# Causal attention: the mask on the scores' diagonal blocks moves from TensorE products to GpSimd selects on the exponentials

## The reference

```
sa, ca, ga, sb, cb, gb = (mod[:, 0], ..., mod[:, 5])
h = _layernorm(x) * (1 + ca) + sa
q, k, v = heads(Wq, bq), heads(Wk, bk), heads(Wv, bv)          # 16 heads of 16
att = einsum('bhtd,bhsd->bhts', q, k) * scale
att = where(causal, att, -inf)
y = einsum('bhts,bhsd->bhtd', softmax(att), v) -> (B, T, C) @ Wp + bp
x = x + ga * y
h = _layernorm(x) * (1 + cb) + sb
x = x + gb * ffn(h)                                            # two layers, untouched
```

## Time and profile before

| | |
|---|---|
| time, 3 runs | 4161.38 us median, 4150.5 to 4162.23 |
| profiled execution | 4156.13 us, its span 4154.3 us |
| busy in the span | PE 3759.8 (91%), DVE 3079.0 (74%), ACT 2612.0 (63%), POOL 1887.2 (45%) |
| mean granted PE clock | 0.964 |
| L728 ACT exponentials | 768, 610.9 us busy; 528.5 us idle before them, 371.7 of it until L869 |
| L907 / L882 / L924 PE | 1536 / 1536 / 3072 products |

### The profile page before, as it was taken

How to read it: one execution, slowest core, us unless ns; L and a number is a source line. 1 busy time by engine, 2 the same in 40 slices (tenths; PEclk the granted TensorE clock), 3 DMA queues, 4 the chain that set the end, 5 groups by cost and what they waited for, 6 DMA issues and landing times.

```text
span 4154.3 us, 88049 instructions
## 1 busy us (share of the span) xinstructions
PE 3759.8 (91%) x33070; PEld 2895.4 (70%) x33070; DVE 3079.0 (74%) x7229; ACT 2612.0 (63%) x5759; POOL 1887.2 (45%) x1444
## 2 busy tenths in 40 slices
PE   4799999999998759999999999989999999999997
PEld 2354545445544347888888888878888888888886
DVE  4677777777776358777787877777888788788884
ACT  1355555555555447777777777767777777767774
POOL 1212322232233035555555555555666565656664
PEclk7799999999999879999999999999999999999999
DMA  4444244353441120000000000011000000000000
GB/s 124 88 74 119 58 112 102 73 125 75 92 128 34 33 67 31 15 20 18 17 20 15 20 17 18 17 43 41 22 28 27 23 26 22 26 24 25 24 23 21
DMA packets 146019, 195.93 MB, mean 47 GB/s; under 512 B 21596, under 2 KB 119608, under 8 KB 145600
## 3 DMA queue, kind: packets, MB, share of 16 engines
q1 hardware_dynamic: 145600, 190.31, 18.4%
HBM read 113.66 MB, written 67.16 MB: 44 GB/s over the span
## 4 chain that ended last, share of the span: by engine, by line
PE 24%; DVE 14%; ACT 12%; DMA 8%; issue 5%; POOL 0%; DVEq 0%; SPq 0%; POOLq 0%; ACTq 0%
PE b_bank_m L1914 10%; DMA b_hs<-b_fr 8%; PE b_bank_p L1914 5%; ACT b_e L1794 4%; DVE b_e L2142 3%; PE b_bank_et L1979 2%; PE b_bank_t L1914 2%; DVE b_qk_rot L2111 2%; ACT L1837 2%; DVE b_rot L2115 2%; PE b_bank_ot L1994 2%; PE b_bank_s L1968 1%; ACT b_e_t L1804 1%; DVE b_ag L2206 1%; ACT b_ag L1829 1%
## 5 line engine op out<-in xcount | busy, mean ns | idle before, releaser
L728 ACT ACTIVATE a_e_t<-a_ring 128x1024 f32<-128x1024 f32 (+3 forms) x768 | 610.9, 809 | 528.5 <-PE a_ring L869 371.7
L1050 DVE TENSOR_REDUCE a_mx<-a_ring 128x2 f32<-128x1024 f32 (+3 forms) x768 | 724.5, 956 | 233.8 <-PE a_ring L869 113.1
L1682 POOL TENSOR_TENSOR b_e<-b_e,b_share 128x512 f32<-128x512 f32 (+1 forms) x512 | 505.9, 991 | 801.2 <-DVE b_share L2150 801.1
L1794 ACT ACTIVATE b_e<-b_e,b_bias 128x256 f32<-128x256 f32 (+1 forms) x1024 | 494.2, 486 | 164.7 <-DVE b_bias L2142 163.8
L2142 DVE CUSTOM_DVE_ANT_0 b_e<-b_bank_s,b_mask,b_inv 128x256 f32<-128x256 f32 (+1 forms) x1024 | 415.8, 460 | 31.1 <-PE b_bank_s L1968 31.1
L1667 POOL TENSOR_TENSOR b_qk_rot<-b_qk_rot,b_rot 128x512 f32<-128x512 f32 x256 | 351.7, 1384 | 130.1 <-DVE b_rot L2115 130.1
L1804 ACT ACTIVATE b_e_t<-b_bank_et 128x512 f32<-128x512 f32 (+1 forms) x512 | 287.2, 561 | 184.2 <-PE b_bank_et L1979 184.1
L882 PE MATMUL a_ring<-a_k_st,a_q_st 48*128 48x512 f32 (+3 forms) x1536 | 328.2, 424 | 77.4 <-ACT a_e_t L728 41.6
L907 PE MATMUL a_ring<-a_q_st,a_k_st 50*128 50x512 f32 (+3 forms) x1536 | 340.0, 441 | 40.7 <-ACT a_e_t L728 13.7
L907 PEld LDWEIGHTS a_ring<-a_q_st,a_k_st 50*128 50x128 f32 x1536 | 147.5, 189 | 298.0 <-issue 145.0
L1979 PE MATMUL b_bank_et<-b_ident,b_e 128*128 128x128 f32 x1920 | 310.8, 282 | 43.1 <-ACT b_e_t L1804 43.1
(11 more groups left out here) (238 smaller groups left out, 11010.3 us busy)
## 6 DMA issues: line engine op xcount, KB each, us to landing
a_q_st<-a_parts_q SPq DMA_DIRECT2D x192, 128.0 KB, 4.8
a_k_st<-a_parts_k SPq DMA_DIRECT2D x192, 128.0 KB, 7.5
a_parts_q<-a_qk_p SPq DMA_DIRECT2D x16, 1024.0 KB, 8.0
a_parts_k<-a_qk_p SPq DMA_DIRECT2D x16, 1024.0 KB, 8.1
b_fl<-f_rows SPq DMA_DIRECT2D x64, 256.0 KB, 4.1
a_xl<-in_L_attn_x SPq DMA_DIRECT2D x9, 1024.0 KB, 5.3
a_x<-in_L_attn_x SPq DMA_DIRECT2D x8, 1024.0 KB, 9.3
x_rows<-a_x SPq DMA_DIRECT2D x8, 1024.0 KB, 4.6
```

The lines of the kernel that those rows point to most:

```text
L728: act.activation(e_t[:, step % 2, 2 * pair:2 * pair + 2, 0:cols], slot[:, :].rearrange("p (h t) -> p h t", h=2)[:, :, 0:cols], ACT.Exp).th ...
L1050: dve.reduce_max(mx[:, g % 2, :, pair, piece, t:t + 1], slot[:, :].rearrange("p (r c) -> p r c", r=2)[:, :, 0:cols], AX.X)\
L1682: pool.tensor_tensor(weights, weights, share[:, h % SPS, 2 * j:2 * j + 2].unsqueeze(2) .broadcast_to([P, 2, 2 * WIN - lo]), ALU.mult).then ...
L1794: ins = act.activation(weights, weights, ACT.Exp, scale=-1.0, bias=bias[:, h % SPS, at:at + 1], accum_out=total[:, h % SPS, at:at + 1])
```

## The change

The scores of the second pass get no mask products any more: L869 with `mask_st`, four for each pair of each diagonal step, 2048 in all. The exponential is taken of unmasked scores in the triangle. Then POOL sets the masked half of the first 128 columns of both heads to zero in `e_t`, with one `affine_select` per pair (`clear_future`), and `meet_values` of a diagonal step waits for both (`cleared`). The first pass keeps its mask.

POOL's other work, until now in a few long instructions, is cut into pieces and put between the selects by step: 16 scale pieces (8 `tensor_scalar` of 256 columns, 4 products and 4 sums of 512), at `PIECES_AT`, for the f rows of the turn before in group 1 and for x in group 3; the bias in four pieces in steps 8 to 11 of group 2; the sums with the output in steps 6 and 8 of group 0, each half in two instructions. The f rows of a turn are thus modulated in group 1 from step 1 to step 11, and the bias comes in group 2, after the load that follows them. The table `mask_st`, its `memset` and its two selects go, as do the signals `x_scaling` and `f_scaling`. The two waits on `const_made` for 16 become 13.

```
@@ -258,6 +258,15 @@
 STEPS1 = score_steps()
 NSTEP = len(STEPS1)
 LAST = G1 - 1
+DIAGONALS = [n for n, (half, s) in enumerate(STEPS1) if s >= 4 * half]
+NDIAGONAL = len(DIAGONALS)
+
+SCALE_PIECES = 16
+SCALED = 12
+PIECES_AT = (0, 1, 1, 1, 2, 2, 2, 2, 1, 1, 1, 2)
+BIAS_AT = ((2, 8), (2, 9), (2, 10), (2, 11))
+ROWS_AT = ((0, 6), (0, 8))
+assert sum(PIECES_AT) == SCALE_PIECES and len(PIECES_AT) == NSTEP
...
-        mask_st = sb("a_mask_st", [P, 2, P], BF16)
...
-        x_scaling = sig("a_x_scaling", 1)
-        x_scaled = sig("a_x_scaled", 2)
+        x_scaled = sig("a_x_scaled", SCALED)
...
+        cleared = sig("a_cleared", 2 * G1 * NDIAGONAL)
...
-            pool.memset(mask_st[:, :, :], 0.0).then_inc(const_made, 1)
...
-                for m, op, fill, sign in ((ident_h, ALU.not_equal, 1.0, 1), (mask_ts, ALU.is_ge, MASKED, 1),
-                                          (mask_st, ALU.is_ge, MASKED, -1)):
-                    pool.wait_ge(const_made, 10 + 3 * r + (0 if m is ident_h else 1 if m is mask_ts else 2))
+                for m, op, fill in ((ident_h, ALU.not_equal, 1.0), (mask_ts, ALU.is_ge, MASKED)):
+                    pool.wait_ge(const_made, 9 + 2 * r + (0 if m is ident_h else 1))
                     pool.affine_select(out=m[rows, :, :], in_=m[rows, :, :], compare_op=op, fill=fill, base=0,
-                                       pattern=[[64 * sign, 2], [-sign, P]], channel_multiplier=sign)\
-                        .then_inc(const_made, 1)
+                                       pattern=[[64, 2], [-1, P]], channel_multiplier=1).then_inc(const_made, 1)
...
-            def modulate(dst, src, name, shift, scale, scaling, scaled, done, a):
+            def modulate(dst, src, name, shift, scale, scaled, done, k, a):
 
                 aggr, rstd = norms[name]["aggr"], norms[name]["rstd"]
-                pool.wait_ge(rstd_of[name].sem, rstd_of[name].at(a, 1))
-                pool.sem_inc(scaling.sem, 1)
-                for t in range(TB):
-                    ins = pool.tensor_scalar(dst[:, t, :], src[:, t, :], aggr[:, t, 0:1], rstd[:, t:t + 1],
-                                             ALU.subtract, ALU.mult)
-                ins.then_inc(scaled.sem, 1)
-                pool.wait_ge(scaled.sem, scaled.at(a, 1))
-                pool.tensor_tensor(dst[:, :, :], dst[:, :, :], scale.broadcast_to([P, TB, C]), ALU.mult)\
-                    .then_inc(scaled.sem, 1)
-                pool.wait_ge(scaled.sem, scaled.at(a, 2))
-                pool.tensor_tensor(dst[:, :, :], dst[:, :, :], shift.broadcast_to([P, TB, C]), ALU.add)\
-                    .then_inc(done.sem, 1)
-
-            def modulate_x(a):
-                pool.wait_ge(mod_in_loaded.sem, mod_in_loaded.at(a, 1))
-                modulate(xl, xl, "x", mod_in[:, 0:1, :], mod_in[:, 1:2, :], x_scaling, x_scaled, h_ready, a)
-
-            pool.sem_inc(x_scaled.sem, 2)
-            pool.sem_inc(x_scaling.sem, 1)
-            modulate_x(1)
-
-            def body(i, closing=False):
-                pool_steps.start(pool, i)
-                pool.wait_ge(mod_loaded.sem, mod_loaded.at(i, 1))
-                pool.wait_ge(xr_loaded.sem, xr_loaded.at(i, 1))
-                pool_steps.step(pool.tensor_tensor(gate_bp[:, 0, :], modb[:, 0, :], b_p[:, :], ALU.mult))
-                pool.tensor_tensor(x1[:, :, :], x1[:, :, :], gate_bp[:, :, :].broadcast_to([P, TB, C]),
-                                   ALU.add).then_inc(biased.sem, 1)
-                if not closing:
-                    modulate_x(i + 2)
+                ts = slice(2 * (k % 4), 2 * (k % 4) + 2)
+                if k < TB:
+                    pool.wait_ge(rstd_of[name].sem, rstd_of[name].at(a, 1))
+                    pool.tensor_scalar(dst[:, k, :], src[:, k, :], aggr[:, k, 0:1], rstd[:, k:k + 1],
+                                       ALU.subtract, ALU.mult).then_inc(scaled.sem, 1)
+                elif k < SCALED:
+                    pool.wait_ge(scaled.sem, scaled.at(a, TB))
+                    pool.tensor_tensor(dst[:, ts, :], dst[:, ts, :], scale.broadcast_to([P, 2, C]), ALU.mult)\
+                        .then_inc(scaled.sem, 1)
+                else:
+                    pool.wait_ge(scaled.sem, scaled.at(a, SCALED))
+                    ins = pool.tensor_tensor(dst[:, ts, :], dst[:, ts, :], shift.broadcast_to([P, 2, C]), ALU.add)
+                    if k == SCALE_PIECES - 1:
+                        ins.then_inc(done.sem, 1)
+
+            def modulate_x(k, a):
+                if k == 0:
+                    pool.wait_ge(mod_in_loaded.sem, mod_in_loaded.at(a, 1))
+                modulate(xl, xl, "x", mod_in[:, 0:1, :], mod_in[:, 1:2, :], x_scaled, h_ready, k, a)
+
+            def modulate_f(k, a):
+                modulate(f_t, x1, "f", modb[:, 1:2, :], modb[:, 2:3, :], f_scaled, f_done, k, a)
+
+            def clear_future(g, n, a):
+
+                for pair in range(2):
+                    _, _, back, k = slot_of(("s", g, n, pair))
+                    pool.wait_ge(back.sem, back.at(a, k + 1))
+                    block = e_t[:, (g * NSTEP + n) % 2, 2 * pair:2 * pair + 2, 0:P]
+                    pool.affine_select(out=block, in_=block, compare_op=ALU.is_ge, fill=0.0, base=0,
+                                       pattern=[[0, 2], [1, P]], channel_multiplier=-1).then_inc(cleared.sem, 1)
+
+            def add_bias(q, i):
+                if q == 0:
+                    pool_steps.start(pool, i)
+                    pool.wait_ge(mod_loaded.sem, mod_loaded.at(i, 1))
+                    pool.wait_ge(xr_loaded.sem, xr_loaded.at(i, 1))
+                    pool_steps.step(pool.tensor_tensor(gate_bp[:, 0, :], modb[:, 0, :], b_p[:, :], ALU.mult))
+                    pool_steps.end()
+                ts = slice(2 * q, 2 * q + 2)
+                ins = pool.tensor_tensor(x1[:, ts, :], x1[:, ts, :], gate_bp[:, :, :].broadcast_to([P, 2, C]), ALU.add)
+                if q == 3:
+                    ins.then_inc(biased.sem, 1)
+
+            def add_rows(p, i):
                 pool.wait_ge(biased.sem, biased.at(i, 1))
-                for p in range(1 if closing else 2):
-                    pool.wait_ge(gated.sem, gated.at(i, 2 * p + 2))
-                    half = slice(4 * p, 4 * p + 4)
-                    pool.tensor_tensor(x1[:, half, :], x1[:, half, :], f_t[:, half, :], ALU.add)\
-                        .then_inc(x1_done.sem, 1)
-                if closing:
+                pool.wait_ge(gated.sem, gated.at(i, 2 * p + 2))
+                for q in range(2):
+                    ts = slice(4 * p + 2 * q, 4 * p + 2 * q + 2)
+                    ins = pool.tensor_tensor(x1[:, ts, :], x1[:, ts, :], f_t[:, ts, :], ALU.add)
+                ins.then_inc(x1_done.sem, 1)
+
+            def program(mode, i):
+                if mode == "lead":
+                    for k in range(SCALE_PIECES):
+                        modulate_x(k, 1)
+                for g, a in groups(mode, i):
+                    for n in range(NSTEP):
+                        if n in DIAGONALS:
+                            clear_future(g, n, a)
+                        before = sum(PIECES_AT[:n])
+                        for k in range(before, before + PIECES_AT[n]):
+                            if g == 1 and i > 0:
+                                modulate_f(k, i - 1)
+                            if g == 3 and mode == "body":
+                                modulate_x(k, i + 2)
+                        if (g, n) in BIAS_AT:
+                            add_bias(BIAS_AT.index((g, n)), i)
+                        if mode == "body" and (g, n) in ROWS_AT:
+                            add_rows(ROWS_AT.index((g, n)), i)
+                if mode == "closing":
+                    add_rows(0, i)
                     rows, shape = f_t[:, END:TB, :], [P, TB - END, C]
                     pool.wait_ge(end_scaled, 1)
                     pool.tensor_tensor(rows, rows, modb[:, 2:3, :].broadcast_to(shape), ALU.mult)\
                         .then_inc(end_scaled, 1)
                     pool.wait_ge(end_scaled, 2)
                     pool.tensor_tensor(rows, rows, modb[:, 1:2, :].broadcast_to(shape), ALU.add).then_inc(end_done, 1)
-                else:
-                    modulate(f_t, x1, "f", modb[:, 1:2, :], modb[:, 2:3, :], f_scaling, f_scaled, f_done, i)
-                pool_steps.end()
-
-            for i in range(turns - 1):
-                body(i)
-            body(turns - 1, closing=True)
+
+            pool.sem_inc(x_scaled.sem, SCALED)
+            run(pool, program)
 
...
-                    diagonal = P * s >= 512 * half
...
-                                       q_st[rows, 2 * g + pair, lo:lo + cols], start=True, stop=not diagonal)
-                    if diagonal:
-                        mm = add_mask(slot, 0, mask_st, ((0, 64), (0, P)))
+                                       q_st[rows, 2 * g + pair, lo:lo + cols], start=True, stop=True)
                     mm.then_inc(filled.sem, 1)
...
```

(13 more changed lines are left out.)

2 lines of the change are left out of this document (1 added, 1 removed).

## The result

The changed kernel took 4216.9 us (median of 4 runs, 4211.2 to 4233.8) beside 4155.9 for the kernel before in the same rounds: a ratio of 1.0156, 95% interval [1.0118, 1.0195]. It is slower, by 61 us where +4 was forecast, and lies above the range. The profiled execution has a span of 4217.4 us, 63 above that of before.

What follows compares the result with a forecast made beforehand. Most attention steps were taken as bound by a loop of exponential, first-pass product, value products, scores and mask. Seven turns of (2.1 + 1.3 - 3.1) give +2.1, ends +1.5, called +4: 4165 us, range 4138 to 4200.

Steps and rivals of the forecast that it cites:

- The mask's removal: Second-pass diagonal steps on PE: 0.11 or 0.07 us gained each, 3.1 us a turn; at the ends 2.2 and about 2.4.
- The selects and the queue: Value products waiting for GpSimd lose 2.1 us a turn, queueing behind pieces 1.3; the last steps lose 5.5 and 0.6.
- chain: From the second exponential's end through one select to the value products on PE: 0.15 + 0.40 + 0.06 = 0.61 us.
- the wake: Delay on GpSimd before a select starts: 0.15 us, since its fill value is moved to a register after the wait.
- PE's release: Delay from the select's end to the value products on PE: 0.06 us, taken as ACT's.
- A piece: GpSimd's other work, cut up: a scale piece 1.22 us, an add 1.19, plus some 0.06 of gap.
- the columns: In GpSimd's select, 128 more columns cost 0.11 us, about 0.9 ns each; the skill's rule would make them about twice as dear.
- The sum: Whole kernel: seven turns +2.1 us and the ends +1.5, so +3.6, called +4; the attention stage gives back its gain.
- Rivals 1 and 2: GpSimd links the loop, chain about 0.66, 4179 to 4193, chance 0.25; strided select 0.62, about 4230, chance 0.06.
- rival 4: Diagonal steps: mask worth 0.14 us in most, pieces fall into PE's own waits; -17 us, 4144, chance 0.22.
- rival 3: Group 2: PE's new waits lower its clock to a mean of 0.90, 3.3 us more in each of 7 turns; 4188, chance 0.05.
- Dips in group 2: Sign in the changed profile: falls of PE's granted clock in group 2 would make the forecast wrong upward; no size given.

Runs made afterwards that it cites:

- e3: Changed kernel with the second pass's mask products kept, GpSimd's work in pieces, no selects and no wait on them: 4151.8 us, ratio 0.9992.
- h1: Changed kernel without its selects and the value products' wait on them, so no mask on the diagonal blocks: 4151.3 us, ratio 1.0007.
- e2: Kernel before with the second pass's mask products taken out and nothing in their place: 4147.7 us, ratio 0.9991.
- e1: Changed kernel with the second pass's mask products put back beside the selects: 4200.7 us, ratio 1.0105.
- h4: Changed kernel with each select clearing only the first 32 of 128 columns, all waits kept: 4187.4 us, ratio 1.0080.
- e4: Changed kernel with mask products put back for the first pair of each diagonal step only: 4218.3 us, ratio 1.0160.
- h2: Changed kernel with selects left out in steps 10, 11 and 0 alone, no mask there: 4176.5 us, ratio 1.0065.
- k2: Changed kernel with mask products instead of selects in steps 10, 11 and 0, and GpSimd's pieces moved off steps 10 and 11: 4187.6 us, ratio 1.0107.
- v1: Kernel before with the value products moved behind the second scores of the next step: 4249.7 us, ratio 1.0228.

## Why the prediction was wrong, point by point

**The mask's removal** was put at 3.1 us a turn and about 4.6 at the ends, 26 us in all. e3 to h1 is 29.2 at full, before to e2 26.6, and 30 to 31 over all runs: about right.

**The selects and the queue** were put at 2.1 + 1.3 us a turn and 6.1 at the ends, 30 us. Measured from h1 to the changed kernel: 26 to 29. The parts: select 0.40, measured 0.407; chain 0.61, measured 0.62. Two errors inside it cancel: the wake is 0.07, not 0.15 (the gap between two setup selects was the wrong row: in the trace each of those follows a MOVE of 0.03 us that carries the wait, and the selects in place wait themselves), and PE's release 0.14, not 0.06. A piece was put at 1.25 with its gap; its record is 1.28, but a select starts 1.23 after a piece does. Step 0 of group 2 did wait 0.80, and the last group grew by 2.0 us (36.07 to 38.09) where the last 32 us were to grow by 3.

By groups it was less exact than the total says. At the full clock group 2 went from 33.23 to 34.02 where no change was forecast, and group 3 from 38.00 to 37.07. In group 2 selects and queue cost 34.02 - 32.41 = 1.61 us where 0.77 + 0.12 was put. That these misses cancel is luck.

On the columns: 407 - 240 ns for 192 columns is 0.87 ns each, the 0.9 of the prediction. The Trainium skill ("GPSIMD Engine Reference", Performance pitfalls for Q7 kernels) has 2.03 cycles an element for a body that compares and selects, and 1.03 for one unrolled by two. By an estimate at that page's 1.2 GHz (Specifications) these are 1.69 and 0.86 ns: the trace disagrees with the first by about a factor of two and agrees with the second.

**The sum**, +4 us, was near for the schedule: at full the stage went from 1267.8 to 1266 to 1269, and over all runs the schedule is 2 us shorter. Rivals 1 and 2 (a chain of 0.66 or more, a costlier select) are refuted by 0.62 and 0.407, rival 4 (17 us shorter) by the schedule.

**The step that failed** is the clock. The sum has no term for it; it stood only as rival 3, at a chance of 0.05 and a price of 23 us (7 x 3.3), with the argument "the new waits are mostly 0.1 to 0.2 us". The runs show 68 us there. The kind of loss was right, the size a third of what it was, and only one half of the cause was looked at. First, it counted the new waits only, one by one. But the change also takes 2048 products from PE, and a product removed was priced by the time that it had held up the next, as if the clock stood fixed. Taken out alone they bring 90 to 108 us more low (e2, h1), more than the selects bring beside all the products (e1, 43; e3, -4). Windows of PE over the 10 us ahead of group 2's first value products, changed kernel and then before (us, PE busy (x), PEclk, DMA share, GB/s):

```profile
377.00:387.00 10.00, 8.10 (x84) 1.00 0.03 7
546.40:556.40 10.00, 8.38 (x86) 0.94 0.04 8
728.30:738.30 10.00, 8.13 (x84) 1.00 0.03 6
894.57:904.57 10.00, 8.18 (x85) 0.94 0.02 6
```
```profile
379.30:389.30 10.00, 9.03 (x116) 1.00 0.34 111
706.70:716.70 10.00, 9.52 (x122) 1.00 0.34 111
```

PE's busy time there fell from 9.0 to 9.5 us to 8.1 to 8.4. (The DMA share fell too, as the f rows now go 5 us later; e1 has 0.02 to 0.03 in the same place and keeps its clock, so that alone is not the cause.) The prediction had the steps of this stretch before it and gave the products in them no part in the clock. Second, the price: a mean of 0.90 in group 2 is 0.2 x 33.2 x 7 = 46 us at the low level, at 0.50 us each. The runs have 219 to 224 us more, at 0.31 each: the price of a microsecond was too high and the amount nearly five times too small. In the trace group 2 is at 0.61 in two turns of seven and at 0.93 or more in the others, and group 3 has low stretches in most turns. "Dips in group 2" stood among the signs of being wrong upward, and they came.

**What the runs show, and what not.** Shown: the loss is time at the 1.2 GHz level. In low time over the kernel before, all runs: the products away, 90 and 108 us (e2, h1); the selects with all products in place, 43 (e1); a short select without them, 163 (h4); the selects without them, 222 to 224. The two together bring more than their sum.

Not shown: what decides whether a given group falls. The four windows of the changed kernel above are alike within 0.3 us, two lead into a low group and two do not (the 0.94 of those two is the low stretch beginning). In e4 PE is busy 8.3 of the 10 us ahead of group 2 in six turns, and 5, 19, 5, 19, 5 and 5 us low follow; h1 has 8.3 ahead of it in two turns and stays within 3 us low after both. A late load of the maxima stands ahead of four long stretches at that seam (h2, k2 twice, and e2, where PE waited 0.99 us and 18 us low follow), but h1 waited 0.84 and 0.96 us for it and did not fall, and v1 waits 1.7 us in all for DVE at that place in every turn and falls in two of seven, for 10 us. No run held the load's landing fixed. I leave this open.

The Trainium skill ("TensorE: Matmul & The Clock Gate", Why this matters for your kernels) warns of idle gaps between bursts of products. No long one stands in the stage: the longest wait of PE from 150 to 1500 us, changed kernel, is 1.6 us (waits of PE):

```profile
PE a_ring L941 <- DVE a_mx L1084: 20.6, 32, 1.6
PE a_outp L958 <- POOL a_e_t L664: 17.9, 30, 1.4
```

The clock was lost with 2048 small products missing and many short waits added, and with no single long gap.

## What to carry to other kernels

A small product on TensorE may be worth more than its time: before you remove it from a stage that already has low stretches (101 us here), price the stage at the low level too, group by group, and not only the new waits one by one. Split any difference into schedule and clock before you explain it; two turns of one kernel at different clocks give the exchange rate (here 0.31 us per us), and the mean clock of every run gives the split without a profile. Do not judge a clock by one execution: here it moved by 80 us from one to the next. A right sum of schedule terms says little when the change also moves the clock.

## What was not expected of the hardware

- The same 265 products of a group take 34.02 us or 44.79 in one execution, with no difference in the program.
- The removal of 2048 products, worth 26 to 31 us of schedule, gave no time clear of noise even with nothing in their place (e2 0.9991, h1 1.0007 of the kernel before).
- From the end of a select to the start of the value products that it releases pass 0.14 us; from an exponential to the select, 0.07.
